# A two-layer graph kernel: another layout for the first message stage, and a quarter of the second layer's row gathers made by TensorE

## What is computed

```python
xs = concat([x[src, :8], x[dst, :8]])                    # 16 scalars
xv = concat([x[src, 8:], x[dst, 8:]])                    # 16 vectors
y1, y2 = sph(edge_vec)                                   # direction
h = sqrt(2) * relu(emb @ W1 / sqrt(10))                  # 10 -> 16
w = (h @ W2 / 4).reshape(E, 7, 16, 8)                    # 7 weight blocks per edge
s_out = PW_S * (einsum('eu,euw->ew', xs, w0) + INV_SQRT3 * einsum('eui,ei,euw->ew', xv, y1, w1))
g_out = ...  # the same with w2, w3
v_out = ...  # xs*y1 with w4, xv with w5, xv*y2 with w6
msg = concat([GAIN * tanh(s_out), GAIN * tanh(g_out)[:, :, None] * v_out]) * norm
x = layernorm(x + segment_sum(msg, dst))

e = leaky(x[src] @ a[:32] + x[dst] @ a[32:])             # layer two
ex = exp(e - segment_max(e, dst)[dst])
x = layernorm(x + segment_sum(x[src] * (ex / segment_sum(ex, dst)[dst]), dst))
```

## Time and profile before

| | |
|---|---|
| time, median of three runs | 6777.66 us (6775.47 to 6781.96) |
| profiled execution, its own time | 6777.46 us |
| its span, first to last instruction | 6775.7 us |
| busy: PE / DVE / ACT / POOL | 3333.0 / 3454.1 / 2603.3 / 4873.7 us |
| granted TensorE clock, mean of the span | 0.785 |

### The profile page before, as it was taken

How to read it: one execution, slowest core, us unless ns; L and a number is a source line. 1 busy time by engine, 2 the same in 40 slices (tenths; PEclk the granted TensorE clock), 3 DMA queues, 4 the chain that set the end, 5 groups by cost and what they waited for, 6 DMA issues and landing times. The chain is left out here.

```text
span 6775.7 us, 55327 instructions
## 1 busy us (share of the span) xinstructions
PE 3333.0 (49%) x12859; PEld 1618.4 (24%) x12859; DVE 3454.1 (51%) x4317; ACT 2603.3 (38%) x3635; POOL 4873.7 (72%) x4419
## 2 busy tenths in 40 slices
PE   0008999999999999999999990000000000000000
PEld 0004444444444444444444440000000000000000
DVE  5326877888888888788888872011111111111112
ACT  0006776666666666666666660000000000000000
POOL 4467777777777777777777726777777777777775
PEclk9999999999999999999999995555555555555555
DMA  3511111111111111111111100011111111111111
GB/s 143 181 36 26 32 32 30 31 31 27 31 29 31 31 28 30 30 31 31 27 31 29 25 12 17 13 26 26 25 25 25 25 25 25 25 25 25 25 25 24
DMA packets 266125, 228.08 MB, mean 34 GB/s; under 512 B 181312, under 2 KB 242565, under 8 KB 263406
## 3 DMA queue, kind: packets, MB, share of 16 engines
q0 software_dynamic: 121824, 79.09, 8.0%
q1 hardware_dynamic: 144082, 147.06, 6.7%
HBM read 137.59 MB, written 88.34 MB: 33 GB/s over the span
## 5 line engine op out<-in xcount | busy, mean ns | idle before, releaser
L1159 POOL DMA_INDIRECT gxb<-tab_d,idxb x1600 | 1699.1, 1062 | 518.0 <-issue 518.0
L541 POOL DMA_INDIRECT gx<-in_x,idx x1540 | 1673.5, 1087 | 411.3 <-issue 374.8
L868 DVE TENSOR_TENSOR prod<-G_ps,hid 128x1000 f32<-128x1000 f32 x1200 | 1422.8, 1193 | 640.5 <-PE G_ps L744 298.1
L758 PE MATMUL R_ps<-sums,red 128*48 128x500 f32 x2400 | 1295.1, 623 | 0.0
L1257 PE MATMUL R_ps<-dm,ones 125*125 125x125 f32 x2 | 0.8, 494 | 2522.2 <-DVE dm L1286 2522.2
L1199 DVE TENSOR_TENSOR lk<-sdf,gxb 125x40 f32<-125x40 f32 x40 | 9.5, 238 | 1877.3 <-DMA gxb<-tab_d,idxb 1877.3
L637 ACT ACTIVATE FT<-T_ps 128x500 fp32r<-128x500 f32 x1200 | 707.2, 589 | 522.0 <-PE T_ps L727 323.2
L727 PE MATMUL T_ps<-ident,HL 125*128 125x125 f32 x4800 | 752.3, 280 | 252.6 <-ACT HL L631 172.1
L548 POOL TENSOR_TENSOR sums<-prod 128x500 f32<-128x500 f32 x400 | 502.1, 1255 | 514.2 <-DVE prod L868 303.4
L1166 ACT ACTIVATE wx<-ex 125x40 f32<-125x40 f32 x40 | 9.5, 238 | 1835.0 <-issue 1657.6
L727 PEld LDWEIGHTS T_ps<-ident,HL 125*128 125x128 f32 x4800 | 573.5, 143 | 467.4 <-ACT HL L631 172.4
(11 more groups left out here) (199 smaller groups left out, 4163.5 us busy)
## 6 DMA issues: line engine op xcount, KB each, us to landing
y_d<-zrb SPq DMA_DIRECT2D x40, 664.1 KB
gx<-in_x,idx POOLq DMA_INDIRECT x1600
gxb<-tab_d,idxb POOLq DMA_INDIRECT x1600
xd_d<-zeros SPq DMA_DIRECT2D x16, 1562.5 KB
xv<-xd_d SPq DMA_DIRECT2D x40, 625.0 KB
y_d<-zr SPq DMA_DIRECT2D x40, 625.0 KB
em<-in_edge_attr SPq DMA_DIRECT2D x40, 195.3 KB
kp<-keep_d SPq DMA_DIRECT2D x40, 156.2 KB
```

The costliest lines, as they stand in the source:

```text
L541: nc.gpsimd.indirect_dma_start(out=gx[h][:, c * DIM:(c + 1) * DIM], out_offset=None, in_=x, in_offset=bass.IndirectOffsetOnAxis(idx[h][:, ...
L758: last = Tn.matmul(R_ps[0:NOUT, 0:GW], red[:, i * NOUT:(i + 1) * NOUT], sums2[k][:, i * GW:(i + 1) * GW], start=(i == 0), stop=(i == 2))
L868: V.tensor_tensor(prod[i][:, :].rearrange("p (a e) -> p a e", a=2), gv, hid[k][:, :].rearrange("p (a e) -> p a e", a=2), ALU.mult).then_in ...
L1159: nc.gpsimd.indirect_dma_start(out=gx[h][:, c * T1:(c + 1) * T1], out_offset=None, in_=tab_d, in_offset=bass.IndirectOffsetOnAxis(idx[h][: ...
```

## The change

It has two parts.

**The message stage is laid out anew.** The features of a node are re-ordered once, in preparation, and stored as the table `xp_d`. GpSimd gathers rows of it straight into a ring of ten slots with eight columns each, where they stay as the row of 96 features; all source indices stay on the chip. An edge's features are now in two sets of rows instead of three, 0 to 63 and 64 to 127 of a turned tile: two times four transposes a group instead of three. A product becomes four matmuls over 64 rows each, high and low weights by upper and lower half. The hidden values fill 128 rows once, so that one relu copy does. The sum over two halves of a product moves from VectorE and GpSimd to TensorE: the reduction is six fp32 matmuls with 32 columns of weights, three places in the array by two halves. GpSimd keeps only gathers; its product with the gates goes to VectorE, as do the sums along the direction. `pace` makes GpSimd wait, at every second column, for what the other engines have reached.

**In the second layer 10 of 40 columns come from TensorE.** The node table stays on chip as a high and a low part (`tb`), built between the layers. Node n is in one of 4 x 125 partition rows and one of 25 places. SyncE brings the node numbers of ten columns to all partitions. VectorE compares them with a partition's number (`one_hot`), which makes matrices with a single one per edge. TensorE multiplies them with the table (`column`, 16 matmuls), which gives the 25 candidates of an edge, and adds with two more a number far below zero to all but one. VectorE takes the maximum of each 25 (`pick`). GpSimd gathers the other 30 columns and waits for picked columns at its tenth and its twentieth.

Preparation also sorts out the node numbers for this. The end is the same but for names of semaphores. The diff, cut to its core:

```diff
+    PW = 2 * GT
+    PC = C // PW
+    RING = 2 * PC
...
-    NT = 3
...
+    NT = 2
...
+    XC = 10
+    CG = C - XC
+    NG4 = 4
```

The message stage, first GpSimd, then TensorE, then VectorE:

```diff
-                    def add(n, k):
-                        pool.wait_ge(S("b_mul"), n * 3 + 1)
-                        if not isinstance(n, int) or n > 1:
-                            pool.wait_ge(S("b_R"), n - 1)
-                        nc.gpsimd.tensor_tensor(sums2[k][:, 0:GW], prod[0][:, 0:GW], prod[0][:, GW:2 * GW], ALU.add).then_inc(S("b_addp"), 1)
...
+                    def pace(p, c):
+                        if c == 0:
+                            hold(S("b_lo"), p + 1)
+                        if c == 2 and (not isinstance(p, int) or p > 2):
+                            hold(S("b_gs"), p * 2 - 4)
+                        if c == 4:
+                            hold(S("b_al"), p + 2)
+                        if c == 6 and some(p):
+                            hold(S("b_mul"), p * 6 - 4)
...
+                    def hidden(n, k):
+                        pe.wait_ge(S("b_FT"), n * NT + 1)
+                        for l in range(2):
+                            last = Tn.matmul(T_ps[0][:, 0:GW], wh[64:128, l * 128:(l + 1) * 128], FT[k][64:128, 0:GW], start=(l == 0), stop=(l == 1))
+                        last.then_inc(S("b_H"), 1)
...
                             pe.wait_ge(S("b_mul"), n * 3 + i - 1)
-                        q = G_ps[(k * 3 + i) % 2]
-                        for j in range(2):
-                            w0, g0 = (2 * i + j) * 128, j * 512
-                            if i < 2:
-                                last = Tn.matmul(q[:, g0:g0 + GW], wst[:, w0:w0 + 128], FT[k][:, i * GW:(i + 1) * GW], start=True, stop=True)
-                            else:
-                                w0 = (4 + 2 * j) * 128
-                                Tn.matmul(q[:, g0:g0 + GW], wst[:, w0:w0 + 128], FT[k][:, 0:GW], start=True, stop=False)
-                                last = Tn.matmul(q[:, g0:g0 + GW], wst[:, w0 + 128:w0 + 256], FT[k][:, 2 * GW:3 * GW], start=False, stop=True)
+                        for l in range(2):
+                            for a in range(2):
+                                c0 = 0 if i == 2 and a == 1 else GW
+                                last = Tn.matmul(G_ps[(k * 3 + i) % 2][:, a * 512:a * 512 + GW], wst[a * 64:(a + 1) * 64, (2 * i + l) * 128:(2 * i + l + 1) * 128],
+                                                 FT[k][a * 64:(a + 1) * 64, c0:c0 + GW], start=(l == 0), stop=(l == 1))
                         last.then_inc(S("b_G"), 1)
 
-                    def reduce(n, k, i):
-                        if i == 0:
-                            pe.wait_ge(S("b_addp"), n + 1)
-                            if some(n):
-                                pe.wait_ge(S("b_rt"), n)
-                        else:
-                            pe.wait_ge(S("b_add"), n + 1)
-                        last = Tn.matmul(R_ps[0:NOUT, 0:GW], red[:, i * NOUT:(i + 1) * NOUT], sums2[k][:, i * GW:(i + 1) * GW], start=(i == 0), stop=(i == 2))
-                        if i == 2:
-                            last.then_inc(S("b_R"), 1)
+                    def reduce(n, k):
+                        pe.wait_ge(S("b_mul"), n * 3 + 3)
+                        if some(n):
+                            pe.wait_ge(S("b_rt"), n)
+                        for a in range(2):
+                            for i in range(3):
+                                last = Tn.matmul(R_ps[32 * i:32 * i + 32, 0:GW], red[:, a * KF:(a + 1) * KF], prod[k][i][:, a * GW:(a + 1) * GW], start=(a == 0), stop=(a == 1))
+                        last.then_inc(S("b_R"), 1)
 
...
                         for c in range(GT):
-                            last = Tn.transpose(Y_ps[0:P, (k * GT + c) * NOUT:(k * GT + c + 1) * NOUT], rt[k][:, c * P:(c + 1) * P], ident[0:NOUT, 0:NOUT])
+                            last = Tn.transpose(Y_ps[0:P, (k * GT + c) * NOUT:(k * GT + c) * NOUT + 96], rt[k][:, c * P:(c + 1) * P],
+                                                ident[0:96, 0:96].rearrange("p (i a f) -> p a i f", a=4, f=MO))
```

```diff
+                        nv = dr[h][:, c0 * 3:(c0 + PW) * 3].rearrange("p (c a u) -> p c a u", a=3, u=1).broadcast_to([P, PW, 3, 8])
+                        for d in range(2):
+                            ev = slot(s)[:, :, d * SD + 16:d * SD + 40].rearrange("p c (a u) -> p c a u", a=3)
+                            last = V.tensor_tensor(tmp[:, :].rearrange("p (c d a u) -> p c d a u", d=2, a=3, u=8)[:, :, d], ev, nv, ALU.mult)
+                        last.then_inc(S("b_tv"), 1)
...
-                        if some(n):
-                            if i == 0:
-                                dve.wait_ge(S("b_addp"), n)
-                            else:
-                                dve.wait_ge(S("b_add"), n)
+                        if i == 0 and later(n):
+                            dve.wait_ge(S("b_R"), n - 1)
                         gv = G_ps[(k * 3 + i) % 2][:, :].rearrange("p (a e) -> p a e", a=2)[:, :, 0:GW]
-                        V.tensor_tensor(prod[i][:, :].rearrange("p (a e) -> p a e", a=2), gv, hid[k][:, :].rearrange("p (a e) -> p a e", a=2), ALU.mult).then_inc(S("b_mul"), 1)
-
-                    def add(n, k):
-                        dve.wait_ge(S("b_mul"), n * 3 + 3)
-                        if not isinstance(n, int) or n > 1:
-                            dve.wait_ge(S("b_R"), n - 1)
-                        q = prod_t[:, 2 * GW:].rearrange("p (i a e) -> p i a e", i=2, a=2)
-                        V.tensor_tensor(sums2[k][:, GW:3 * GW].rearrange("p (i e) -> p i e", i=2), q[:, :, 0], q[:, :, 1], ALU.add).then_inc(S("b_add"), 1)
```

The second layer, GpSimd, TensorE and VectorE:

```diff
+                            for c in range(CG):
+                                if c in (10, 20):
+                                    pool.wait_ge(S("d_red"), (t * 2 + h) * 2 * XC + 2 * NS + 4 * (c - 5) // 10)
+                                    pool.sem_inc(S("go"), 1)
...
+                    def column(ch, h, j):
+                        q = ch * XC + j
+                        if j == 0:
+                            pe.wait_ge(S("d_hot"), ch * 5 + 5)
+                        pe.wait_ge(S("d_red"), q * 2 + 2)
+                        slot = SLOTS[(h * XC + j) % NS]
+                        for l in range(2):
+                            for g in range(NG4):
+                                for (f0, f1, w), ps in zip(FUS, slot):
+                                    nc.tensor.matmul(ps[0:PE2, 0:w], hot[h][:, g * XP + j * P:g * XP + j * P + PE2],
+                                                     tb[l][:, g * GS + f0 * KL:g * GS + f0 * KL + w], start=(l == 0 and g == 0), stop=False)
+                        for (f0, f1, w), ps in zip(FUS, slot):
+                            last = nc.tensor.matmul(ps[0:PE2, 0:w], hotk[h][:, j * P:j * P + PE2], far[:, 0:w], start=False, stop=True)
+                        last.then_inc(S("d_col"), 1)
+
...
+                    def one_hot(ch, h, t):
+                        dve.wait_ge(S(f"d_nd{h}"), t * 32 + 32)
+                        if not isinstance(ch, int):
+                            dve.wait_ge(S("d_col"), (ch - 1) * XC)
+                        for g in range(NG4):
+                            V.tensor_scalar(hot[h][:, g * XP:(g + 1) * XP], nodes[h], iot[:, g:g + 1], None, ALU.is_equal).then_inc(S("d_hot"), 1)
+                        V.tensor_scalar(hotk[h][:, 0:XP], nodek[h], iot[0:KL, 0:1], None, ALU.is_equal).then_inc(S("d_hot"), 1)
+
+                    def pick(ch, h, j):
+                        dve.wait_ge(S("d_col"), ch * XC + j + 1)
+                        slot = SLOTS[(h * XC + j) % NS]
+                        for (f0, f1, w), ps in zip(FUS, slot):
+                            V.tensor_reduce(gx[h][0:P, (CG + j) * T1 + f0:(CG + j) * T1 + f1],
+                                            ps[0:P, 0:(f1 - f0) * KL].rearrange("p (f k) -> p f k", k=KL), AX.X, ALU.max).then_inc(S("d_red"), 1)
...
                         for h in range(2):
                             chunk(h, t)
+                            one_hot(t * 2 + h + 2, h, t + 1)
+                            for j in range(XC):
+                                pick(t * 2 + h + 1, 1 - h, j)
+                    chunk(0, PAIRS - 1)
```

865 lines of the change are left out of this document (457 added, 408 removed).

## The result

| | before | after |
|---|---|---|
| median of four runs each | 6776.57 us (6768.99 to 6781.96) | 6680.42 us (6665.98 to 6689.13) |
| ratio, 95% interval | | 0.986 (0.983 to 0.988) |
| span of the profiled execution | 6775.7 us | 6669.5 us |

The prediction was 5880 us with a range of 5380 to 6680. The sign is right, the size is not: 96 us were won of 897, and the median stands at the upper end of the range, just outside. Later runs gave a second number. On another chip, on which the kernel before takes 6637.49 us, the changed kernel takes 5130.11. Both have to be explained.

What follows compares the result with a forecast made beforehand. The prediction took TensorE to bound the message stage and GpSimd's issue the second layer. 6777.5 - 532 (message stage) - 372 (second layer) + 10 (around) = 5883.5, so 5880 us, range 5380 to 6680.

Steps and rivals of the forecast that it cites:

- waits and clock dips: Message stage before: of 8.84 us a group, 7.8 taken as TensorE's work and 1.0 as waits and clock dips.
- The message stage, TensorE: TensorE's work per group after the change: transposes, hidden, products and reduction sum to 7.29 us, ends 5.83 and 11.33.
- 7 half-steps of 12: Message stage reduction: neighbouring column places overlap, two records of one place cannot pass; six matmuls take 5.82 x 7/12 = 3.40 us.
- rival 1: Message stage: tiles overlap fully, TensorE 5.83 and VectorE the bound at 6.5 us a group; 5480 us in all, chance 0.12.
- 0.2 us of waits: Message stage: pauses in heavy groups, added to TensorE's 7.29 us to give 7.5 us a group.
- The second layer, GpSimd: GpSimd bounds a chunk at 46 us: 30 gathers 37.5, disturbance 5.5, one-hots 3; ends 43 and 50; -372 us in all.
- Rival 3: Second layer: VectorE's one-hots and picks block gathers in full, 59 us a chunk; 6400 us in all, chance 0.08.
- The slow clock: Second layer: granted clock, 0.50 before, counted on to rise with TensorE busy 36 of 46 us; at 0.50 ten columns take 66.
- Rival 2: Second layer: TensorE stays at the lower clock level, 66 for 46 us a chunk; 6680 us in all, chance 0.11.
- sum of 42.5: Second layer: chain of VectorE and TensorE per chunk, 42.5 us with 3.5 for a slow start, below GpSimd's 46.
- Rival 4: Message stage: reduction's column places do not overlap, 5.82 us, group 9.9; 6845 us, or 7480 with products serial too; chance 0.09.
- Around: Outside the two loops: preparation +5 us for re-ordering and node selection, between the layers +5 (0 to 15 each).

Runs made afterwards that it cites:

- kind A: Chips on which the kernel before, timed beside the others, takes 6774 to 6783 us (chips 2, 6, 11 and that of the first result).
- kind B: Chips on which the kernel before, timed beside the others, takes 6637 to 6650 us (chips 10 and 15).
- b_only: The changed kernel with its second layer as before (40 gathers a chunk, no one-hots, picks or columns), on kind B: 5572.42 us, 0.839 of before.
- few_rows: The changed kernel with the matmuls of a column over 32 rows in place of 125, same number of matmuls, on kind B: 5955.19 us.
- after_5: The changed kernel once more, unaltered, on kind B: 5130.11 us against 6637.49 for the kernel before, ratio 0.773.

## Why the prediction was wrong

**The step that was missing.** The sum has TensorE, VectorE and GpSimd bound one another only by their semaphores, their engines' times and the 5.5 us that a chunk's work on VectorE costs the gathers (one beside the 2.46 us product took 2.50 for 0.94). On kind A GpSimd's gathers also hold TensorE back: in the second layer, once they stand in a row, TensorE goes on for some 75 matmuls and then gets less than one a gather (16 in 26.7 us, at a gather every 1.25). The prediction has no term for this: it put it at nothing, without a reason. Its size is the difference of the kinds: 63.1 - 41.4 = 21.7 us a chunk, 870 us, and 7.73 - 6.11 = 1.62 us a group, 650 us.

In the trace of before it could not be seen in the second layer, where TensorE did nothing. Nor does it fill the 1.0 us of "waits and clock dips" of the message stage. There TensorE idles 21 us behind "issue" from 1000 to 2900 us, 0.1 us a group. And the kernel before takes 138 us more on kind A than on kind B, of which its second layer has some (55.5 - 52.7) x 40 = 112, if it runs on kind B as in `b_only`; that leaves at most 26 us for the message stage, an estimate of 0.07 us a group. So the loss in this stage came with the new layout, and the wrong step was to carry the engines' times over to it as if nothing but semaphores tied them.

**The message stage, TensorE.** The terms were near where rows gave them: four product matmuls 1504.12 - 1503.46 = 0.66 for 0.54, transposes 0.57 and 0.48 for 0.52. The overlap of the column places was mis-sized: six reductions take 1503.46 - 1501.65 = 1.81 us; I took 3.40, between 1.94 and 5.82. So the three places overlap here: 1.81 is less than the 1.94 of perfect overlap, and the 7 half-steps of 12 behind my 3.40, an estimate, are not what the trace shows. A group without pauses is 1526.42 - 1520.65 = 5.77 us, against my lower end of 5.83.

**VectorE.** Predicted were 6.5 us a group, and in rival 1 VectorE as the bound. On kind B the stage runs at 6.11, and the bound is TensorE: it is busy 1816 of 1900 us and VectorE 1723, which is 5.54 us a group. Half of the groups come at 5.8 us or less, TensorE's 5.77; about one in eleven takes over 8.5, where TensorE stands up to 6.0 us for a multiplication. So rival 1 had the overlap right and the bound wrong:

```profile
1000.00:2900.00 1900.00, 1816.12 (x11736) 931.07 (x11730) 1723.42 (x2780) 1121.05 (x2130) 1227.97 (x1347) 0.97 0.19 43
...
L864 DVE TENSOR_TENSOR prod<-G_ps,hid 128x1000 f32<-128x1000 f32 x927 | 1071.6, 1191 | 99.7 <-issue 65.8 <-PE G_ps L756 32.7
```

VectorE idles 99.7 of 1900 us ahead of its multiplications and 177 in all. The low part costs 0.551 twice per two groups, 0.55 a group for my 0.7; and its instructions overlap a little (927 multiplications of 1.191 are 1104 us, in 1071.6 of busy time), so that durations added up, as in my sum, are more than busy time. The 0.2 us of waits that I added are 6.11 - 5.77 = 0.34 on kind B and 7.73 - 5.77 = 1.96 on kind A.

**The second layer, GpSimd.** On kind B it is the bound as predicted, at 41.4 us for 46. Thirty gathers are 37.5; the rest is 3.9, where I had 5.5 for the chunk's work and 3 for one-hots:

```profile
4129.27 3.23 POOL L1199 DMA_INDIRECT gxb<-tab_d,idxb  x1 [0.30 <-issue]
4132.81 1.03 POOL L1199 DMA_INDIRECT gxb<-tab_d,idxb  x1 [0.30 <-issue]
4134.14 2.04 POOL L1199 DMA_INDIRECT gxb<-tab_d,idxb  x1 [0.30 <-issue]
```

One gather of 3.23 stands beside the product; those beside the one-hots, which run from 4135.2 to 4139.2, take 2.04, 1.25 and 1.25, and the next three, beside picks, 0.95 each. Four one-hots are 3.21 and a pick 1.08, a column 3.8: predicted were 4.2, 1.1 and 3.6. These hold on both kinds. Rival 3 (gathers blocked by picks) is out.

**The slow clock.** Rival 2 gives 6680 us, the very time measured, and is still wrong; that its number fits is luck. In the chunk above the granted clock is 0.50 only around the crawl (5206.2 to 5233.5) and 1.00 outside it, and on kind B it is 0.95 from 3400 to 5000 us. What it would look like `few_rows` shows: 0.50 throughout with TensorE always busy, 61.9 us a chunk on kind B. The 3.5 us for a slow start in the sum of 42.5 no run shows. `after_5` has, from 3400 to 4950 us, 26 stretches at 0.50 of 3.4 or 6.8 us; in the one of 4014.6 to 4021.4, behind 2.45 us of waiting for a pick, the 16 matmuls of a column take 5.87 us, two columns later 3.32. So such a start cost 2.6 us there, and without the 3.5 the sum is 39.0, below GpSimd's 46 all the same.

**Rival 4** (places one after another) is out: 1.81 for 5.82.

**Around.** Predicted were +10 us outside the two loops and +4 for the start-up. On kind A it was +42 (20.1, 21.1 and 0.4 from above), on kind B -4.5, against the trace of before, which is of kind A.

So 5880 describes neither kind. With the measured pitches in it the same sum gives some 5140 us on kind B and 6660 on kind A. On kind B the mechanism of the second layer was right and both stages were cheaper than predicted (6.11 for 7.5, 41.4 for 46), so that 5130 lies below the range; on kind A the missing step more than ate this up. That 5880 lies between the two is luck.

## What to carry to other kernels

A sum of engine times says nothing of how two engines bear on each other that were never dense at the same time in the trace of before; where a change first sets them side by side, give this a term or a rival of its own. Where GpSimd gathers without pause beside a TensorE that runs many small matmuls, try waits in the rows of gathers, tied to TensorE's progress: in the second layer a wait at every second gather was worth 644 us on kind A (6651.68 to 6007.35, chip 11) and cost 114 on kind B (chip 10). It is no full cure: the message stage has such waits and still loses 1.6 us a group on kind A. And run a change on more than one chip: here the same pair of kernels has a ratio of 0.986 on one kind and 0.773 on the other.
